# Two cross-attention layers: context normalised by rows in layer 0, and its split parts transposed by DMA in both

## The reference

```python
kn = layer_norm(ctx, ln1_g, ln1_b)
K = (kn @ wk + bk); V = (vn @ wv + bv)            # layer 0
kh = (ctx @ Wk); vh = (ctx @ Wv)                  # layer 1
```

## Time and profile before

| | |
|---|---|
| Times of the runs shown, us | 1605.43, 1613.99, 1622.47 (median 1613.99) |
| Span of the profiled execution, us | 1604.4 |
| The profiled execution's own time | not given apart; the lowest run is 1.0 us above the span |
| Busy, share of the span | PE 88%, PEld 56%, DVE 58%, ACT 42%, POOL 27% |
| Mean granted TensorE clock | 0.949 |
| DMA | 149.59 MB, queue of SP busy 33.5% of 16 engines |

### The profile page before, as it was taken

The page is one execution under the profiler, slowest core; times in us unless marked ns, Lnnn a source line. Parts: engine busy times, 40 slices in busy tenths (PEclk is TensorE's granted clock), DMA queues, the critical chain, the costliest instruction groups (busy, mean ns, idle before and its releaser), DMA issues. The chain is left out here.

```text
span 1604.4 us, 34148 instructions
## 1 busy us (share of the span) xinstructions
PE 1418.0 (88%) x12908; PEld 900.5 (56%) x12908; DVE 935.5 (58%) x1677; ACT 666.4 (42%) x1294; POOL 431.3 (27%) x487
## 2 busy tenths in 40 slices
PE   5497898899999756999959999999999999999968
PEld 3255566566656532544435666666666666666653
DVE  5856788798887747622343555454544454555444
ACT  1324565566555534421122444444444444444441
POOL 3212444455443445020000111111111111111124
PEclk9798999999999766999979999999999999999979
...
DMA packets 117005, 149.59 MB, mean 93 GB/s; under 512 B 51056, under 2 KB 92528, under 8 KB 113776
## 3 DMA queue, kind: packets, MB, share of 16 engines
q1 hardware_dynamic: 116848, 147.34, 33.5%
...
## 5 line engine op out<-in xcount | busy, mean ns | idle before, releaser
L642 POOL TENSOR_TENSOR attn_probs<-attn_p,attn_probs 128x400 f16<-128x400 f32 x192 | 188.1, 980 | 915.1 <-ACT attn_probs L993 914.9
L1112 DVE TENSOR_REDUCE attn_nmax<-attn_p_max 100x1 f32<-100x722 f32 x256 | 231.3, 904 | 109.2 <-PE attn_p_max L839 102.8
L817 PE MATMUL attn_p_proj<-attn_ctxT,kv_w_k 128*128 128x361 f16 x1536 | 251.6, 319 | 21.7 <-DMA attn_ctxT<-ctxT_parts 18.2
L822 PE MATMUL attn_p_proj<-kv_w_v,attn_ctxT 128*128 128x512 f16 (+1 forms) x1152 | 264.3, 379 | 0.0
L983 ACT ACTIVATE attn_p<-attn_p_sc,attn_score_bias 128x400 f32<-128x400 f32 x192 | 113.5, 591 | 299.4 <-PE attn_p_sc L868 298.6
L817 PEld LDWEIGHTS attn_p_proj<-attn_ctxT,kv_w_k 128*128 128x128 f16 x1536 | 145.4, 98 | 107.9 <-DMA attn_ctxT<-ctxT_parts 18.6
L993 ACT CAST attn_probs<-attn_p 128x400 f16<-128x400 f32 (+1 forms) x384 | 197.8, 516 | 0.0
L822 PEld LDWEIGHTS attn_p_proj<-kv_w_v,attn_ctxT 128*128 128x128 f16 (+1 forms) x1152 | 110.4, 101 | 111.0
L642 DVE TENSOR_TENSOR attn_probs<-attn_p,attn_probs 128x400 f16<-128x400 f32 (+1 forms) x192 | 119.9, 625 | 89.2 <-ACT attn_probs L993 88.5
L983 ACT ACTIVATE attn_p<-attn_p_sc 128x400 f32<-128x400 f32 x192 | 95.8, 499 | 152.4 <-PE attn_p_sc L864 150.0
L822 PE MATMUL attn_p_proj<-l_w_v,attn_ctxT 128*128 128x512 f16 (+1 forms) x576 | 136.2, 388 | 0.8 <-DVE attn_vbuf L1159 0.8
...
## 6 DMA issues: line engine op xcount, KB each, us to landing
...
attn_kstack_a<-attn_knat SPq DMA_DIRECT2D x128, 180.5 KB, 3.5
...
attn_kstack_b<-attn_knat SPq DMA_DIRECT2D x64, 180.5 KB, 3.6
attn_c<-in_ctx_dram SPq DMA_DIRECT2D x40, 256.0 KB, 3.2
...
```

The lines of the kernel that those rows point to most:

```text
L642: eng.tensor_tensor(probs[:r, g % 2, 1, t, :HG * SQ], p32[:r, t % 3, :], probs[:r, g % 2, 0, t, :HG * SQ], ALU.subtract).then_inc(p_lo_mad ...
L817: last = pe.matmul(bank[:, :HALF], w_k[:, wa, k, c0 + m * P:c0 + (m + 1) * P], ctxT[:, par, ca, k, n * HALF:(n + 1) * HALF], **flags)
L822: last = pe.matmul(bank[:r, :], ctxT[:, par, ca, k, P * t:P * t + r], w_v[:, wa, k, c0:c0 + E], **flags)
L1112: dve.tensor_reduce(nmax[:SQ, hh:hh + 1], p_max[:SQ, :, :HALF], AX.XY, ALU.max, negate=True).then_inc(max_made, 1)
```

## The change

- Layer 0: `c32` has six buffers, so all tiles of a batch are loaded a step ahead. VectorE takes the statistics in slots 0 to 5 (`stat`), POOL the power in slot 6, and VectorE subtracts the mean and multiplies by 1/std in place (`ctx_norm`), one slot before ACT's cast. The cast stands at slots 8, 10, ... 18. The scaled identities, the broadcast by TensorE, `rrow` and `kscaled` go. ACT evacuates each K bank with bias and scale into `k32` (f32) and that frees the bank; ACT's cast and VectorE's lo part read `k32`. The broadcasts' constant goes too.
- Both layers: the transposes on TensorE and the copy out of PSUM go. SP issues a transposing DMA for each tile, from `cparts` (two buffers) to `ctxT`, whose last tile is padded from 82 to 96 rows. A cast waits until the transpose of the tile two before it has landed (`c_moved`), the first projection of a unit until all six have.
- The store to HBM and layer 1's loads of it go. Layer 1 loads the raw context, casts, subtracts and transposes it for every unit, so twice for a batch, with two buffers for `c32` and two for `cparts`, both laid over a weight tensor that is free by then.
- On SP's queue the transposes stand between the K stackings, the loads behind transposes; SP's steps are no longer a loop.

```diff
 KT = -(-SK // P)
 KROWS = [min(P, SK - P * t) for t in range(KT)]
...
-        self.ctx = {2: 0, 6: 1, 12: 2, 14: 3, 17: 4, 20: 5} if layer == 0 else {}
-        self.var_t, self.diag_t = 19, 20
-        self.bc = {22: 0, 23: 1} if layer == 0 else {}
+        self.stat = {t: t for t in range(KT)} if layer == 0 else {}
+        self.var_t = KT
+        self.ctx = {8: 0, 10: 1, 12: 2, 14: 3, 16: 4, 18: 5} if layer == 0 else {0: 0, 1: 1, 4: 2, 5: 3, 7: 4, 8: 5}
...
+            rstd = sc.sb("rstd", [P, KT])
+            k32 = sc.sb("k32", [P, 2, SK])
+        else:
+            flat = spare[:].rearrange("p a k n -> p (a k n)")
+            c32 = flat[:, :4 * E].bitcast(F32).rearrange("p (i n) -> p i n", i=2)
+            cparts = flat[:, 4 * E:].rearrange("p (i a n) -> p i a n", i=2, a=2)
...
+            def load_ctx_tile(u, b, t):
+                if not (isinstance(u, int) and u * KT + t < NC):
+                    sp.wait_ge(c_lo_made, u * KT + (t + 1 - NC))
                 r = KROWS[t]
-                sp.dma_start(c32[:r, t % 3, :], ctx_d[bass.ds(b, 1), P * t:P * t + r, :].rearrange("o p e -> (o p) e")
-                             ).then_inc(c_loaded[t % 3], 16)
-
-            def spill_ctx(b, par):
-                sp.wait_ge(misc_freed, sl.misc_count(b - 1, ("ctx", KT - 1)))
-                sp.dma_start(ctxT_d[bass.ds(b, 1)].rearrange("o p n -> (o p) n"), ctxT[:, par].rearrange("p a k s -> p (a k s)")
-                             ).then_inc(ctxT_moved[par], 16)
-
-            def load_ctxT(u, par, b):
-                if not (isinstance(u, int) and u < 2):
-                    sp.wait_ge(proj_ready, NPROJ * (u - 1))
-                sp.dma_start(ctxT[:, par].rearrange("p a k s -> p (a k s)"), ctxT_d[bass.ds(b, 1)].rearrange("o p n -> (o p) n")
-                             ).then_inc(ctxT_moved[par], 16)
+                sp.dma_start(c32[:r, t % NC, :], ctx_d[bass.ds(b, 1), P * t:P * t + r, :].rearrange("o p e -> (o p) e")
+                             ).then_inc(c_loaded[t % NC], 16)
+
+            def transpose_ctx(u, par, t):
+                r = TROWS[t]
+                sp.wait_ge(c_lo_made, u * KT + (t + 1))
+                sp.dma_start_transpose(ctxT[:, par, :, :, P * t:P * t + r].rearrange("p a k s -> p (a k) s"),
+                                       cparts[:r, t % 2].rearrange("p a n -> p (a n)")).then_inc(c_moved[t % 2], 16)
...
-                    if prep and not (isinstance(s, int) and s == 0):
-                        for t in range(3):
-                            load_ctx_tile(s + 1, t)
                     if proj:
                         load_q(s, par, s)
-                    for i in range(2):
-                        if prep:
-                            load_ctx_tile(s + 1, 3 + i)
-                        if proj:
-                            stack_k(s, par, i)
+                        stack_k(s, par, 0)
                     if prep:
-                        load_ctx_tile(s + 1, 5)
+                        for t in range(3):
+                            transpose_ctx(s + 1, 1 - par, t)
+                    if proj:
+                        stack_k(s, par, 1)
                     if prep:
-                        spill_ctx(s + 1, 1 - par)
+                        for t in range(3, KT):
+                            transpose_ctx(s + 1, 1 - par, t)
+                    if not isinstance(s, int) or s + 2 < U:
+                        for t in range(KT):
+                            load_ctx_tile(s + 2, s + 2, t)
...
-                    load_ctx_tile(0, t)
+                    load_ctx_tile(0, 0, t)
+                for t in range(KT):
+                    transpose_ctx(0, 0, t)
+                    load_ctx_tile(1, 1, t)
...
                 sp.wait_ge(q_stored, 16 * count)
                 place_onehot()
-                steps(sp, step)
-                for i in range(2):
-                    sp.wait_ge(ctxT_moved[i], 16 * (B // 2))
+                for s in range(U):
+                    step(s, s % 2, sl.kind(s))
...
-                def unit(u, par, b, ahead=True):
+                def ahead(u, par, b, t):
+                    transpose_ctx(u, par, t)
+                    if t + NC < KT:
+                        load_ctx_tile(u, b, t + NC)
+
+                def unit(u, par, b, more=True, after=True):
+                    b1 = b + 1 if par else b
                     load_q(u, par, b)
                     for i in range(2):
                         stack_k(u, par, i)
-                    if ahead:
-                        load_ctxT(u + 2, par, b + 1)
-
-                load_ctxT(0, 0, 0)
-                load_ctxT(1, 1, 0)
+                        if more:
+                            ahead(u + 1, 1 - par, b1, 2 * i)
+                            ahead(u + 1, 1 - par, b1, 2 * i + 1)
+                    for t in range(2):
+                        if more:
+                            transpose_ctx(u + 1, 1 - par, 4 + t)
+                        if after:
+                            load_ctx_tile(u + 2, b + 1, t)
+
+                for t in range(NC):
+                    load_ctx_tile(0, 0, t)
+                for t in range(KT):
+                    ahead(0, 0, 0, t)
+                    if t >= KT - 2:
+                        load_ctx_tile(1, 0, t - (KT - 2))
...
+                for u in range(U):
+                    unit(u, u % 2, u // 2, more=u + 1 < U, after=u + 2 < U)
...
-            def ctx_transposes(s, par, t):
-
-                b, r = s + 1, KROWS[t]
...
-                    for k in range(ET):
-                        o = (a * ET + k) * P
-                        last = pe.transpose(misc16[:, o:o + r], cparts[:r, t % 2, a, k * P:(k + 1) * P], ident16[:r, :r])
-                last.then_inc(misc_ready, 1)
-
-            def rstd_rows(s, n):
-
-                pe.wait_ge(rdiag_made, (s + 2) * KT)
...
-                    o = P * (t - 3 * n)
-                    last = pe.matmul(misc32[:, o:o + r], ones32[:r, :], rdiag[:r, t, :r], start=True, stop=True)
-                last.then_inc(misc_ready, 1)
...
                 if a == 0:
-                    if layer == 1:
-                        pe.wait_ge(ctxT_moved[par], 16 * (u // 2 + 1) if isinstance(u, int) else 8 * (u - par) + 16)
-                    else:
-                        pe.wait_ge(misc_freed, sl.misc_count(u - 1, ("ctx", KT - 1)))
+                    for i in range(2):
+                        pe.wait_ge(c_moved[i], 16 * (KT // 2) * u + 16 * (KT // 2))
...
+                if layer == 0:
+                    act.wait_ge(c_normed, u * KT + (t + 1))
+                else:
+                    act.wait_ge(c_loaded[t % NC], 16 * (KT // NC) * u + 16 * (t // NC + 1))
+                if not (isinstance(u, int) and u == 0 and t < 2):
+                    act.wait_ge(c_moved[t % 2], 16 * (KT // 2) * u + 16 * (t // 2))
+                act.copy(cparts[:r, t % 2, 0, :], c32[:r, t % NC, :]).then_inc(c_hi_made, 1)
...
+                    act.wait_ge(proj_ready, NPROJ * u + (a + 1))
                     if layer == 0:
-                        if n == 0:
-                            return
-                        act.wait_ge(proj_freed, NPROJ * u + (a + 1))
-                        cols = slice(0, SK)
-                        src = kscaled[:, m % 2, :]
+                        if n == 0 and not (isinstance(u, int) and 4 * u + m < 2):
+                            act.wait_ge(k_lo_made, 4 * u + (m - 1))
+                        act.activation(k32[:, m % 2, cols], src, ACT.Identity, bias=kb_col[:, m:m + 1],
+                                       scale=1.0 / WS).then_inc(proj_freed, 1)
+                        if n == 1:
+                            act.wait_ge(proj_freed, NPROJ * u + (a + 1))
+                            if m % 2 == 0 and not (isinstance(u, int) and u == 0):
+                                act.wait_ge(stacked[m // 2], 16 * NSTACK * u)
+                            act.copy(knat[:, m, 0, :], k32[:, m % 2, :]).then_inc(k_hi_made, 1)
...
                     act.wait_ge(q_acc_ready, u + 1)
                     if u >= 3:
                         act.wait_ge(q_lo_made, u - 2)
                     act.activation(p32[:, u % 3, :], p_sc[:, u % 2, :QHALF], ACT.Identity, bias=queries[2][:, u // 2:u // 2 + 1],
                                    scale=queries[3]).then_inc(q_made, 1)
-                for n in range(2):
-                    rstd_row(-1, 1, n)
+                    if u >= 3:
+                        ctx_hi(0, u - 3)
+                ctx_hi(0, KT - 1)
                 act.wait_ge(q_lo_made, 2 * ET)
+            else:
+                for t in range(KT):
+                    ctx_hi(0, t)
...
-                dve.tensor_scalar(var[:], mv[:, :, 1], eps, WS * WS, ALU.add, ALU.mult).then_inc(var_made, 1)
...
+                dve.tensor_scalar(var[:], mv[:, :, 1], eps, None, ALU.add).then_inc(var_made, 1)
+
+            def ctx_norm(b, t):
...
                 dve.wait_ge(rstd_made, b + 1)
```

(35 more changed lines are left out.)

183 lines of the change are left out of this document (48 added, 135 removed).

## The result

The changed kernel takes **1776.2 us** (median of 4 runs, 1769.3 to 1780.5) against 1614.7 for the kernel before in the same job: ratio 1.099, 95% interval 1.095 to 1.104. The profiled executions span 1775.1 and 1604.4 us, so there are 170.7 us to find. The forecast was +63.

A forecast was written before the change was run, and what follows sets the result against it. TensorE was taken to bound both layers, VectorE close behind in layer 0. Terms -41 + 63 + 28 + 13 = +63 us gave 1668 profiled, 1677 us on the median; own range 1630 to 1760, with the chances 1590 to 1790.

The forecast's parts named there:

- What bounds the kernel: Both layers: TensorE bounds layer 1, and layer 0 too with VectorE close behind; units of 44.8 us, steps about 58.
- The price of a transposing DMA: Both layers, SP's queue: one 128x1024 tile takes 1.0 us to issue and 4.5 us to land.
- the extrapolated query load: Layer 0's load of 1536 short runs, 0.65 us to issue, 4.4 to land, extended to 8192 pieces.
- the upper ends: Highest price of a transposing DMA, from 8192 assumed pieces: 2.0 us to issue and 10 us to land.
- Layer 1's chain: Layer 1's units: tile 4's late load holds ACT's cast and the evacuation projection 11 needs; 4.5 us a unit, +63 us.
- Layer 0's steps: Layer 0's six steady steps: 6.8 us gained a step, -41 us in all, bounds -18 and -54.
- half of the max waits: Layer 0: half of TensorE's waits for VectorE's row max go, 1.7 us a step.
- the 5.1 forecast: Layer 0: TensorE loses 288 transposes and 78 broadcasts of rstd, 5.1 us a step.
- The starts: Beginnings of both layers get longer: layer 0 +13 us; layer 1 +20 us, and +8 us in its step 0.
- transposes at the lower ends of the price: First rival, both layers: cheap transposes make the change a wash, some 1602 to 1615 us; chance 0.17.
- the second rival: Layer 1: slack in the chain, tile 4 landed by 1030, so projection 11 doesn't wait; near 1582 us, chance 0.17.
- The third: Third rival, both layers: six transposes in series bound the units, 60 us each at 10 us; about 1924 us, chance 0.13.

The follow-up runs named there:

- l1_transposes_first: Changed kernel with layer 1's transposes 0 to 3 and the loads of tiles 2 to 5 ahead of the K stackings on SP: 1766.1 us, 1.092 of before.
- the mended kernel: Changed kernel, layer 0 only: context loads behind their transposes, second K stacking last, normalising to transposes two slots later: 1737.6 us, 1.076 of before.
- l1_plain_copy: Changed kernel with every transposing DMA of layer 1 a plain copy of the same bytes, so nothing is transposed there: 1773.1 us, one run.

## Why the prediction was right or wrong

- **What bounds the kernel**: right. TensorE at a full clock bounded layer 1, and what reached it came through in full, and more than in full. One reading was off: 627 us hold 14.5 units and not 14, so a unit was 43.2 us and not 44.8.
- **The price of a transposing DMA**, 1.0 us to issue and 4.5 to land: measured 1.24 and 3.6 (3.2 in layer 0, 4.1 in layer 1). Right, nearer to the plain load than to the extrapolated query load, as chosen. The 8192 pieces behind the upper ends were wrong: it is 1024 packets. The Trainium skill, VectorE: DVE Perf Modes, "The three transpose paths", gave 10.5 us by my estimate, and the trace speaks against such a sum for a 128x1024 tile. By Advanced Engine Details and Errata, "X-Bar Transpose (TRN2)", they are as fast as regular ones: the landings of 4.1 and 4.3 us agree.
- **Layer 1's chain**: the mechanism was right, place and engines included: tile 4's cast waits for its load ahead of the evacuation that projection 11 needs, 4.05 us where 4.5 stood. Moving the last two tiles alone took a unit to 45.0 us. The term was mis-sized, 7.9 instead of 4.5, and what it left out is not the chain but what comes with it. It priced a pause at its length, while TensorE's matmuls behind it ran slower: 2.5 us of busy time a unit. And 1.3 us are small waits. It also ended the chain at the first late cast; the cast of tile 5, one slot on, waits too, and by l1_transposes_first that one alone keeps a unit at 51.0.
- **Layer 0's steps**: the step that failed, -41 us against +20. That the last transposes "have five slots, some 12 us" was true for the first projection, the only reader that I looked at. ACT reads the same signal earlier: its cast of tile 5 needs buffer 1 back from transpose 3, and that stands behind 9.1 us of stacking. I had said that the stacking "can be late at no cost", and had not asked what it holds up. That wait was only 1.4 us of a step. For the other places there was no term at all: in the order tried, the loads behind their transposes gave 1.2 us more (one run), and 3.0 us came with the later slots, which take normalising and POOL's first low part away from slots 8 and 9. Together the order and the places cost 5.6 us a step, 61.4 against 55.8. Normalising cost 0.92 us for a full tile (0.79 in the mended kernel), where I took 0.6.
- **The size of the gain, once mended**: 58.1 to 55.8 us, 2.3 instead of 6.8. The part that failed is the 1.7 us from half of the max waits: I took the wait of the max for VectorE as a matter of VectorE's load. In 210 to 450 us TensorE's busy time fell by 4.3 us a step, near the 5.1 forecast, but its waits for the max went from 3.5 to 4.1 us a step even in the mended kernel, and all its idle time from 5.0 to 6.9, though VectorE had lost work. The transposes alone bring 3.3 to 3.8 (estimate 21.6/6.5 = 3.3 from TensorE's time). So the normalising ahead, for which the 78 broadcasts go, brings nothing that could be seen; it was not run by itself, and the two kernels differ in the order on SP's queue too.
- **The starts**: right, +15 and +19 against +13 and +20; layer 0's first projection starts at 92.5 us (forecast: a last landing at about 94), layer 1's 25.0 us behind the start of its block (forecast 26).
- **The rivals**: transposes at the lower ends of the price were not the case (1.24 us to issue, not 0.36), and even the plain copies of l1_plain_copy, issued in 0.78, left a unit at 50.7: what stood against this rival, the load behind six stackings, decided. The slack of the second rival was missing by the place of two casts; with them moved, the whole kernel still is at 1.017. The third (transposes as the bound) was wrong in its price.
- **The range**: the prediction names two, 1630 to 1760 and, with its chances, 1590 to 1790. The measured 1776 lies above the first and inside the second. That is no merit of the second: two terms, layer 0's steps by 61 us and layer 1's units by 48, were off in the same direction.
